# A two-layer sequence block on one core: where the last serial stage and the third mixture of experts stand in the queues, and which engine makes the scan's products

## Chip, cores and metric

One NeuronCore of a Trainium2 chip runs the whole kernel in one launch. The metric is device time in microseconds (us). Matmuls run on TensorE (PE in the profile), activations on ScalarE (ACT), elementwise work and scans on VectorE (DVE) and GpSimd (POOL); SyncE (SP) issues the DMAs.

## The reference, cut to what matters

There are 2048 tokens (2 batches of 1024) of 128 features. Each of four steps adds its output to its input and normalises:

```python
# 1: Mamba: 256 channels, 16 states, per batch
xi, res = split(x @ in_proj_w.T); xi = silu(causal_conv4(xi))
dt, Bm, Cm = split(xi @ x_proj_w.T); delta = softplus(dt @ dt_proj_w.T + dt_b)
h = exp(delta * A) * h + delta * Bm * xi      # along time, 256 x 16 states
y = sum_n(h * Cm) + xi * Dp
x = layernorm(x + (y * silu(res)) @ out_proj_w.T)
# 2: a projection of x rounded to fp8
x = layernorm(x + q(x) @ q(w).T + bias)
# 3: a small state space layer with 16 states for all features
x = layernorm(x + scan16(x) @ C.T + D * x)
# 4: mixture of 8 experts (128 -> 256 -> 128), top 2, capacity 512, and a side network for overflow
x = layernorm(x + moe(x))
```

## The kernel before

The tokens are four chunks (`c` = 0 to 3) of 512. A tile is 128 partitions by 512 tokens of float32. For each chunk there are four stages.

**pre** makes the channels `u`, the gate `res_gate`, the rows of B and C (`low`, written to DRAM and read back by SP, broadcast to 128 partitions, as `b_row` and `c_row`, two states per DMA, in rings of `ROWS` = 4), and `delta`.

**scan**: 32 steps `k` (2 halves of the channels by 16 states). For each step GpSimd makes `drive = du * b_row` (ring of 5), ScalarE writes the decay `exp(delta * rate)` into one of three PSUM banks `ps_state`, VectorE scans in that bank (L919), makes `product = state * c_row` (L934; ring of 5), and in the first chunk of a batch first copies the last column to `carry`. TensorE adds each product into `ps_y` with a matmul by the identity (L475). A float32 matmul is two instructions in the trace.

**tail** is a chain of 16 pieces with hardly any width: gate, output projection (L491), three layer norms, the fp8 projection, the small scan, the router (L534), picking experts. Each piece waits for one on another engine. It uses the PSUM banks `ps_g` and `ps_u`, which the mixture of experts uses as well, so a chunk's tail cannot start before the mixture of experts of the chunk before has ended.

**gate, up, join, down, accum** are the mixture of experts ("MoE"): per expert four groups of three matmuls (L564), Gelu on ScalarE (L774), a product on VectorE (L1079), 16 matmuls (L608) and four accumulations on VectorE (L1092). `fin` is the last layer norm.

The order of the work on every engine is written out: `PLACES` has a place for every piece of every stage, `run` sorts them and calls them in that order, and each engine executes its queue strictly in that order, waiting on semaphores. Before, one set of places serves all chunks (the last chunk has some of its own): while chunk c+1 is scanned, chunk c has its tail and then its MoE. After the last scan stand the last tail, alone, and the last MoE. The last MoE has six PSUM banks, the others three.

The expert weights are split into a high and a low part, and a product is three matmuls of parts: ScalarE makes the high part (L677), VectorE the low part (`split`, L887), 16 instructions on each; before, they are spread over the first scan.

ScalarE loads a table set before an Exp or Ln, a Gelu or a Silu when another set is loaded. The program asks for one by hand in two places (`preload_act_table_set`, L651 and L776); the other loads are placed by the compiler.

Of the kernel before, what the change touches and what calls it, by code (L numbers as in the profile page):

```python
# [15 lines left out]
P = 128  # L16
# [9 lines left out]
RANK = 64  # L26
# [10 lines left out]
DRIVES = 5  # L37
PRODUCTS = 5
# [14 lines left out]
for _k, _w in PARAMS.items():  # L53
# [12 lines left out]
        "pre": (-15.5, -15, -14.75, -12.25, -11.25, -11.25, -11.25, -11),  # L66
        "step": (-0.75, -0.25, 0.25, 0.75, 1.25, 1.75, 2.25, 2.75, 3.25, 3.75, 4.25, 4.75, 5.25, 5.75, 6.25, 6.75, 7.25, 7.75, 8.25, 8.75, 9.25, 9.75, 10.25, 10.75, 11.25, 11.75, 12.25, 12.75, 13.25, 13.75, 14.25, 14.75),
        "fin": (35.5,),
    },
    "tensor": {  # L70
        "pre": (-15.985, -15.243, -15.072, -15.009, -15.009, -14.386, -13.697, -12.945),
        "finish": (1.026, 2.077, 2.38, 4.291, 4.768, 4.895, 4.895, 4.895, 5.341, 5.797, 6.224, 6.906, 7.702, 7.702, 7.702, 7.932, 9.319, 10.249, 10.26, 11.316, 11.443, 11.926, 12.585, 12.638, 12.638, 13.422, 15.593, 15.611, 16.065, 16.065, 16.224, 16.652),
        "tail": (16.789, 18.74, 19.78, 20.114, 20.162, 21.02, 21.662, 21.662, 22.551, 22.551, 22.551, 22.589, 23.318, 23.361, 24.693, 25.257),
        "gate": (23.461, 24.08, 25.461, 26.34, 27.782, 28.281, 29.005, 30.66, 31.128),
        "up": (23.536, 25.234, 26.3, 27.395, 27.991, 28.939, 30.472, 30.681, 31.382),
        "down": (26.054, 26.575, 27.518, 28.046, 29.344, 30.584, 30.786, 32.018, 32.195),
# [4 lines left out]
    },  # L81
    "scalar": {
        "pre": (-15.267, -14.377, -14.369, -14.369, -13.882, -13.064, -12.783, -11.823),
        "step": (-1.07, -1.006, 1.488, 1.488, 1.589, 1.611, 2.1, 2.759, 3.153, 3.566, 5.216, 5.216, 5.248, 5.331, 6.088, 6.923, 7.616, 7.907, 8.049, 8.329, 8.329, 9.344, 9.881, 10.805, 10.879, 10.988, 12.125, 12.63, 13.421, 13.719, 14.454, 14.752),
        "tail": (17.732, 18.093, 18.788, 19.301, 19.58, 19.883, 20.439, 20.816, 21.252, 22.002, 22.002, 22.841, 22.982, 23.694, 25.3, 25.697),
        "gate": (24.049, 24.647, 25.608, 26.597, 28.089, 28.166, 29.618, 30.859, 30.859),
        "fin": (34.6366, 37.5376),
        "split": (-16.891, -3.814, -0.051, 3.661, 5.837, 7.947, 11.702, 14.515),
        "tail 3": (15.02, 17.27, 18.506, 20.73, 21.524, 21.524, 21.524, 22.579, 24.535, 25.601, 25.601, 25.601, 25.601, 25.601, 25.741, 26.135),
        "gate 3": (26.08, 26.08, 29.514, 30.153, 30.779, 30.861, 30.901, 31.003, 31.159),  # L90
    },
    "gpsimd": {
        "du": (-7.973, 6.048),
        "step": (-1.518, -1.379, 0.207, 0.207, 0.207, 1.332, 1.422, 1.422, 1.422, 1.422, 3.619, 3.769, 4.649, 4.649, 5.511, 5.678, 6.659, 8.269, 8.87, 9.084, 9.517, 9.517, 9.517, 9.535, 12.453, 13.427, 13.427, 13.427, 13.427, 13.427, 13.427, 13.427),
        "tail": (17.819, 18.848, 20.618, 21.206, 22.833, 23.004, 25.062, 26.086, 26.086, 27.015, 27.015, 27.015, 27.751, 28.224, 28.256, 28.309),
        "tail 3": (13.509, 13.904, 14.945, 16.762, 17.736, 18.242, 18.307, 19.402, 20.434, 21.642, 24.097, 24.097, 24.097, 24.097, 26.965, 27.136),
    },
    "vector": {
        "delta": (-11.192,),
        "step": STEP,  # L100
        "finish": (0.782, 1.228, 1.228, 2.015, 2.578, 2.578, 3.571, 4.267, 4.782, 4.806, 5.472, 6.005, 6.812, 7.405, 7.681, 8.495, 8.687, 8.826, 9.135, 10.111, 11.059, 11.31, 11.938, 12.367, 12.633, 13.353, 13.353, 14.29, 14.539, 15.174, 15.801, 16.001),
        "gated": (9.428, 16.917),
        "tail": (15.554, 18.289, 18.93, 19.521, 20.126, 20.29, 20.721, 20.862, 22.38, 22.562, 22.562, 22.66, 23.827, 23.988, 24.764, 25.633),
        "join": (24.932, 25.56, 26.732, 28.247, 28.753, 29.639, 30.595, 31.702, 31.923),
        "accum": (26.609, 27.363, 28.477, 29.029, 30.366, 30.691, 31.743, 32.226, 32.579),
        "fin": (34.4726, 38.0196),
        "split": (-0.762, 2.312, 4.875, 11.44, 11.64, 13.773, 14.501, 18.497),
# [19 lines left out]
def build(nc, x_t, params, w_gate, w_up, w_down, bc_dram, out):  # L127
    with ExitStack() as ctx:
# [47 lines left out]
        acc = sb("acc", [P, BLOCKS, P])  # L176
        x1 = sb("x1", [P, BLOCKS, P])
# [5 lines left out]
        l1_ln = l1_abs = gelu[:, 0, 0, :]  # L183
        l1_exp = gelu[:, 0, 1, :]
        l1_relu = gelu[:, 1, 0, :]
        l1_sp = l1_t = gelu[:, 1, 1, :]
        l1_step, l1_decay = gelu[0:STATE, 2, 0, :], gelu[0:STATE, 2, 1, :]
        l1_drive = hidden[0:STATE, 1, 0, :]

# [3 lines left out]
        low = sb("low", [RANK + 2 * STATE, 2, CHUNK])  # L193
        sp_abs = sb("sp_abs", [P, HALVES, CHUNK])
        sp_exp = sb("sp_exp", [P, HALVES, CHUNK])
# [7 lines left out]
        product = sb("product", [P, PRODUCTS, CHUNK])  # L203
        carry = sb("carry", [P, HALVES, STATE])
# [11 lines left out]
        l1_state = sb("l1_state", [STATE, 2, CHUNK])  # L216
# [36 lines left out]
        result = sb("result", [P, BLOCKS, P])  # L253
# [27 lines left out]


# [16 lines left out]
        pre_act = Marks(sem("pre_act"), "u0 u1 gate0 gate1 low abs0 relu0 abs1 relu1 exp0 exp1 ln0 ln1")  # L299
        pre_dve = Marks(sem("pre_dve"), "t0 t1 a0 a1 b0 b1 delta0 delta1")  # L300
# [8 lines left out]
        product_dve = sem("product_dve")  # L309
        y_pe = sem("y_pe")  # L310
# [4 lines left out]
        tail_dve = Marks(sem("tail_dve"), "st1 mo1 sh1 r2 st2 mo2 sh2 t a b sp drive scan st3 mo3 vr msq sh3 inv s3 "  # L315
# [21 lines left out]
        def carries(g):  # L337

            c, k = divmod(g, UNITS)
            return c // PER_BATCH * UNITS + k + 1  # L340
# [4 lines left out]
        def run(engine, **parts):  # L345

            places = PLACES[engine]
            order = sorted((STATE * c + at, c, i, k) for i, kind in enumerate(parts)
                           for c in range(1 if kind == "split" else CHUNKS)
                           for k, at in enumerate(places.get(f"{kind} {c}", places[kind])))  # L350
# [11 lines left out]
        def _(sp):  # L362
# [11 lines left out]
            def pair(m, ring, arrived, row, used):  # L374
# [3 lines left out]
                if m >= ROWS:  # L378
                    sp.wait_ge(used, 2 * (m - ROWS) + 2)
                if r == 0:  # L380
                    sp.wait_ge(rows_out, 16 * (c + 1))
                sp.dma_start(ring[:, m % ROWS, :, :],
                             bc_dram[c % 2, None, row + n:row + n + 2, :].broadcast_to([P, 2, CHUNK])).then_inc(arrived[m % ROWS], 16)

            def pre(c, k):
                if k == 4:
# [5 lines left out]
                    sp.dma_start(bc_dram[c % 2], low[RANK:RANK + 2 * STATE, c % 2, :]).then_inc(rows_out, 16)  # L392

            def step(c, k):
                g = c * UNITS + k
                if g == 0:
                    for m in range(ROWS - 1):
                        pair(m, b_row, b_in, 0, drive_pool)
                        if m < ROWS - 2:
                            pair(m, c_row, c_in, STATE, product_dve)  # L400
                if g % 2 == 0:
                    if g // 2 + ROWS - 2 < STEPS // 2:
                        pair(g // 2 + ROWS - 2, c_row, c_in, STATE, product_dve)
                    if g // 2 + ROWS - 1 < STEPS // 2:
                        pair(g // 2 + ROWS - 1, b_row, b_in, 0, drive_pool)
# [11 lines left out]
        def _(pe):  # L417
# [10 lines left out]
            def pre(c, k):  # L428
                if k == 7:
                    return  # L430
# [26 lines left out]
                else:  # L457
                    h = k - 5
                    after(pe, pre_act, c, "low")
                    last = mm(bank_[:, :], dt_proj[0:RANK, h * P:(h + 1) * P], low[0:RANK, q, :], start=True, stop=True)  # L460
                last.then_inc(pre_pe.sem, 1)

            def finish(c, k):
# [10 lines left out]
                pe.wait_ge(product_dve, g + 1)  # L474
                mm(ps_y[:, :], ident, product[:, g % PRODUCTS, :], start=False, stop=(n == STATE - 1)).then_inc(y_pe, 1)  # L475

            def tail(c, k):
                q = c % 2
                b, t0 = tokens(c)
                if k == 0:  # L480
                    if c:
# [3 lines left out]
                    for j in range(BLOCKS):  # L485
                        t = TAPS - 1 + t0 + j * P
                        mm(block_of(ps_u[1][:, :], j), x_in[:, b, t:t + P], ident, start=(j == 0), stop=False)
# [685 lines left out]
```

## Time and profile before

| | us |
|---|---|
| median of 3 runs (lowest, highest) | 533.63 (529.58, 535.17) |
| the profiled execution's own time | 535.09 |
| its span | 533.3 |
| busy in the span: PE, DVE, ACT, POOL | 425.3, 419.7, 315.1, 178.6 |
| mean granted TensorE clock | 0.889 |

The span is the stretch that the trace covers; the time of the same execution is 1.8 us more. An engine's busy time is the union of its instructions; times in the trace count from the start of the span.

### The profile page before, as it was taken

Reading aid. Unit: us, or ns where it says so; the run is one execution under the profiler, and the core shown is the slowest. Engines: PE = TensorE matmul, PEld = TensorE weight load, DVE = VectorE, ACT = ScalarE, POOL = GpSimd, SP = SyncE. Lnnn points to the kernel's source line nnn. Section 1 sums busy time; section 2 is a strip of 40 time slices with the busy share of each in tenths; the row PEclk is TensorE's granted clock in tenths of the full one; section 3 lists DMA queues with packets and bytes.
Section 4 is the critical chain, followed back from the end, with each engine's and each line's share of the span. In section 5 each row is a group of like instructions: output and inputs, shape, how many; then the busy total and the mean of one; then the engine's idle time right before and its main releaser. Section 6 shows DMA issues by size and latency. Waiting matters only on the chain.

```text
span 533.3 us, 5892 instructions
## 1 busy us (share of the span) xinstructions
PE 425.3 (80%) x1680; PEld 256.9 (48%) x1680; DVE 419.7 (79%) x942; ACT 315.1 (59%) x517; POOL 178.6 (33%) x147
## 2 busy tenths in 40 slices
PE   4976667699649999997569999775599995449994
PEld 3322212253235778552245776432367774147883
DVE  3087999997989999698989989978899884334654
ACT  2586552378738976577578785255787832544232
POOL 0056485555163434234163433451534100000000
PEclk9987977799969999999869999969799998656997
DMA  8295768666426354442193554620835000000000
GB/s 300 109 339 175 240 210 263 211 217 202 163 79 200 116 171 161 142 160 78 32 334 133 180 167 132 220 92 20 323 151 175 23 1 1 20 0 1 0 1 20
DMA packets 22064, 74.18 MB, mean 139 GB/s; under 512 B 2320, under 2 KB 4368, under 8 KB 21648
## 3 DMA queue, kind: packets, MB, share of 16 engines
q1 hardware_dynamic: 22032, 73.82, 41.0%
q8 instruction: 13, 0.21, 0.2%
q14 instruction: 19, 0.16, 0.1%
HBM read 72.50 MB, written 1.31 MB: 138 GB/s over the span
## 4 chain that ended last, share of the span: by engine, by line
PE 50%; DVE 21%; issue 13%; ACT 12%; POOL 2%; DVEq 0%; ACTq 0%; POOLq 0%
PE ps_y L475 12%; PE ps_u L608 9%; PE ps_g L564 8%; DVE ps_state L919 6%; PE ps_u L564 5%; DVE product L934 3%; PE ps_state L564 2%; ACT x L703 2%; ACT ps_state L692 2%; DVE stats L944 1%; PE ps_y L608 1%; POOL drive L813 1%; PE ps_g L523 1%; DVE l_state L990 1%; PE ps_g L534 1%
## 5 line engine op out<-in xcount | busy, mean ns | idle before, releaser
L813 POOL TENSOR_TENSOR drive<-du,b_row 128x512 f32<-128x512 f32 x128 | 164.0, 1290 | 208.3 <-DVE ps_state L919 186.0
L475 PE MATMUL ps_y<-product,par 128*128 128x512 f32 x256 | 135.7, 655 | 13.2 <-DVE product L934 12.9
L692 ACT ACTIVATE ps_state<-delta,decay_rate 128x512 f32<-128x512 f32 x128 | 86.2, 687 | 63.9 <-DVE product L934 61.9
L934 DVE TENSOR_TENSOR product<-ps_state,c_row 128x512 f32<-128x512 f32 x128 | 86.1, 680 | 5.5 <-PE ps_y L475 5.3
L919 DVE TENSOR_TENSOR_SCAN ps_state<-ps_state,carry,drive 128x512 f32<-128x512 f32 x64 | 81.5, 1282 | 4.0 <-ACT ps_state L692 4.0
L475 PEld LDWEIGHTS ps_y<-product,par 128*128 128x128 f32 x256 | 48.9, 208 | 70.6 <-issue 37.3
L919 DVE TENSOR_TENSOR_SCAN ps_state<-ps_state,drive 128x512 f32<-128x512 f32 x64 | 77.3, 1219 | 2.3 <-ACT ps_state L692 2.3
L608 PEld LDWEIGHTS ps_u<-wd,hidden 128*128 128x128 f32 x448 | 54.2, 191 | 5.4 <-issue 2.4
L608 PE MATMUL ps_u<-wd,hidden 128*128 128x128 f32 x448 | 54.6, 275 | 0.0
L1092 DVE SCALAR_TENSOR_TENSOR acc<-ps_u,net_weight,acc 128x128 f32<-128x128 f32 x128 | 35.9, 344 | 15.3 <-PE ps_u L608 12.5
L774 ACT ACTIVATE gelu<-ps_g 128x512 f32<-128x512 f32 (+1 forms) x42 | 24.4, 597 | 31.8 <-PE ps_g L564 18.5
L564 PE MATMUL ps_g<-hn_part,wg 128*128 128x512 f32 x114 | 36.2, 439 | 0.3 <-DVE hidden L1079 0.2
L564 PE MATMUL ps_g<-hn_part,wu 128*128 128x512 f32 x108 | 35.9, 450 | 0.2
L622 ACT ACTIVATE var_log<-moments,eps 128x4 f32<-128x4 f32 x16 | 4.8, 298 | 49.2 <-DVE moments L948 42.4
L774 ACT ACT_TABLE_LOAD x25 | 32.1, 1283 | 0.4
L1079 DVE TENSOR_TENSOR hidden<-gelu,ps_g 128x512 f32<-128x512 f32 x36 | 24.0, 679 | 4.9 <-PE ps_g L564 4.7
L564 PEld LDWEIGHTS ps_g<-hn_part,wu 128*128 128x128 f32 x108 | 20.3, 193 | 11.7 <-issue 5.7
L564 PEld LDWEIGHTS ps_g<-hn_part,wg 128*128 128x128 f32 x114 | 21.1, 196 | 8.7 <-issue 2.9
L692 ACT ACT_TABLE_LOAD x18 | 23.1, 1283 | 0.5 <-DVE carry L930 0.2
L564 PE MATMUL ps_u<-hn_part,wu 128*128 128x512 f32 x63 | 19.6, 420 | 2.2 <-ACT gelu L774 2.2
L802 POOL TENSOR_TENSOR du<-delta,u 128x512 f32<-128x512 f32 x8 | 10.5, 1314 | 31.7 <-DVE delta L908 31.7
L445 PE MATMUL ps_g<-x_in,conv_proj 128*128 128x512 f32 x40 | 20.2, 656 | 0.7 <-ACT conv_proj L625 0.7
(199 smaller groups left out, 605.4 us busy)
## 6 DMA issues: line engine op xcount, KB each, us to landing
b_row<-bc_dram SPq DMA_DIRECT2D x64, 512.0 KB, 5.0
c_row<-bc_dram SPq DMA_DIRECT2D x64, 512.0 KB, 4.1
x_in<-x_t SPq DMA_DIRECT2D x4, 256.0 KB, 7.0
gelu<-w_gate SPq DMA_DIRECT2D x1, 1024.0 KB, 9.3
hidden<-w_up SPq DMA_DIRECT2D x1, 1024.0 KB, 10.9
wd<-w_down SPq DMA_DIRECT2D x1, 1024.0 KB, 12.8
out<-result SPq DMA_DIRECT2D x4, 256.0 KB, 2.4
par<-params SPq DMA_DIRECT2D x1, 598.0 KB, 6.7
```

The costliest lines, as they stand in the source:

```text
L445: last = mm(bank_[:, :], conv_proj[:, k, tap, :], x_in[:, b, t0 + tap:t0 + tap + CHUNK], start=(tap == 0), stop=(tap == TAPS - 1))
L475: mm(ps_y[:, :], ident, product[:, g % PRODUCTS, :], start=False, stop=(n == STATE - 1)).then_inc(y_pe, 1)
L564: last = mm(net_bank(c, e, kind, f)[:, :], w_in[kind][wp][:, e, f * P:(f + 1) * P], hn_parts[hp][:, :], start=(i == 0), stop=(i == 2))
L608: last = mm(block_of(out_bank(c, e)[:, :], j), hidden[:, m % 2, f, j * P:(j + 1) * P], wd[:, e, f, :], start=(f == 0), stop=(f == 1))
L692: nc.scalar.activation(ps_state[g % RING][:, :], delta[:, c % 2, h, :], ACT.Exp, scale=decay_rate[:, h, n:n + 1]).then_inc(decay_act, 1)
L703: last = nc.scalar.activation(out_[:, j, :], of(j), ACT.Identity, bias=shifts[:, j:j + 1], scale=scales[:, j:j + 1])
L774: nc.scalar.activation(gelu[0:rows, m % GROUP, f, :], net_bank(c, e, "wg", f)[0:rows, :], ACT.Gelu).then_inc(gelu_act, inc)
L813: nc.gpsimd.tensor_tensor(drive[:, g % DRIVES, :], du[:, h, :], b_row[:, m % ROWS, n % 2, :], ALU.mult).then_inc(drive_pool, 1)
L919: v.tensor_tensor_scan(state[:, :], state[:, :], drive[:, g % DRIVES, :], 0.0 if first else carry[:, h, n:n + 1], ALU.mult, ALU.add).then_ ...
L934: v.tensor_tensor(product[:, g % PRODUCTS, :], state[:, :], c_row[:, m % ROWS, n % 2, :], ALU.mult).then_inc(product_dve, 1)
L1079: v.tensor_tensor(hidden[0:rows, m % 2, f, :], gelu[0:rows, m % GROUP, f, :], net_bank(c, e, "wu", f)[0:rows, :], ALU.mult).then_inc(hidde ...
L1092: last = v.scalar_tensor_tensor(acc[:, j, :], block_of(out_bank(c, e)[:, :], j), net_weight[:, j, e:e + 1], acc[:, j, :], ALU.mult, ALU.add)
```

## The change

- The banks of the last chunk's tail are no longer `ps_g` and `ps_u` but the scan's `ps_state` and `ps_y` (`tail_bank`), and its scratch tiles lie in the ring of products (`l1_of`). It need no longer wait for the third MoE. In the new order the third MoE (c = 2) stands after the last scan, interleaved piece by piece with the last tail; the last MoE follows.
- A quarter of the products (steps 3, 7, 11, ... of every chunk) is made by GpSimd: there the scan writes its result into `drive` in SBUF, and GpSimd multiplies, and in chunks 0 and 2 copies the carry.
- In chunks 1 and 2 GpSimd adds the products of steps 2i and 2i+1, so TensorE adds one tile for two steps.
- The ring of drives has 6 tiles instead of 5, that of products 8 instead of 5. To make room, `low`, `sp_exp` and `l1_state` have one buffer instead of two and `result` shares `acc`. The softplus of `pre` is done for one half of the channels after the other.
- A whole new order, with places of its own for every chunk. All splits of the weights now stand ahead of the first scan, on ScalarE and VectorE. `gate`, `up` and `join` are placed by half of an expert.
- Table sets are asked for ahead of each activation that needs Exp or Ln instead of at two places: 168 requests instead of 14.

```diff
-DRIVES = 5
-PRODUCTS = 5
+DRIVES = 6
+PRODUCTS = 8
+ODD = frozenset(range(1, UNITS, 2))
+PAIRED = (NONE, ODD, ODD, NONE)
+QUARTER = frozenset(range(3, UNITS, 4))
+MULTIPLIED = (QUARTER, QUARTER, QUARTER, QUARTER)
...
+        def tail_bank(c, name):
+            if c == LAST:
+                return {"r1": ps_state[0], "x1t": ps_state[1], "ffn": ps_state[2], "x2t": ps_y, "dlt": ps_state[2],
+                        "bx": ps_state[0], "mean": ps_state[1], "r3": ps_y, "hnt": ps_state[2], "logits": ps_state[1],
+                        "counts": ps_y}[name]
...
             def finish(c, k):          # TensorE
-                pe.wait_ge(product_dve, g + 1)
+                if absorbed(g):
+                    return
+                if paired(g):
+                    pe.wait_ge(pair_pool, count(paired, g))
+                else:
+                    made(pe, g)
...
             def tail(c, k):            # TensorE
                 if k == 0:
-                    if c:
+                    if c == LAST:
+                        pe.wait_ge(product_dve, count(by_vector, STEPS - 1))
+                        pe.wait_ge(state_dve, STEPS)
+                    elif c:
...
             def step(c, k):            # ScalarE
                 if old >= 0:
-                    act.wait_ge(product_dve, old + 1)
-                    if old // UNITS % PER_BATCH == 0:
-                        act.wait_ge(carry_dve, carries(old))
+                    if multiplied(old):
+                        act.wait_ge(state_dve, old + 1)
+                    else:
+                        made(act, old)
...
+                nc.scalar.preload_act_table_set(EXP_LN)
                 nc.scalar.activation(ps_state[g % RING][:, :], delta[:, c % 2, h, :], ACT.Exp,
...
+            def multiply(c, k):        # GpSimd
+                pool.wait_ge(state_dve, g + 1)
+                pool.wait_ge(c_in[m % ROWS], 16 * (m // ROWS + 1))
+                if g >= PRODUCTS:
+                    added(pool, g - PRODUCTS)
+                nc.gpsimd.tensor_tensor(product[:, g % PRODUCTS, :], drive[:, g % DRIVES, :], c_row[:, m % ROWS, n % 2, :],
+                                        ALU.mult).then_inc(product_pool, 1)
+                if c % PER_BATCH == 0:
+                    nc.gpsimd.tensor_copy(carry[:, h, n:n + 1], drive[:, g % DRIVES, CHUNK - 1:CHUNK]).then_inc(carry_pool, 1)
+
+            def pair(c, k):            # GpSimd
+                made(pool, g - 1)
+                made(pool, g)
+                nc.gpsimd.tensor_tensor(product[:, g % PRODUCTS, :], product[:, (g - 1) % PRODUCTS, :],
+                                        product[:, g % PRODUCTS, :], ALU.add).then_inc(pair_pool, 1)
...
             def step(c, k):            # VectorE
-                v.tensor_tensor_scan(state[:, :], state[:, :], drive[:, g % DRIVES, :],
+                v.tensor_tensor_scan(drive[:, g % DRIVES, :] if multiplied(g) else state[:, :], state[:, :], drive[:, g % DRIVES, :],
...
             def finish(c, k):          # VectorE
+                if multiplied(g):
+                    return
```

Here `made(eng, g)` waits for the product of step g from whichever engine makes it, and `added(eng, g)` until it has been used. What the new places give, as the order of the queues: on TensorE and VectorE, scan 0 whole, then tail 0 beside steps 3 to 22 of scan 1, MoE 0 up to step 5 of scan 2, tail 1 beside steps 11 to 30 of scan 2, MoE 1 up to step 14 of scan 3, tail 2 beside the rest of scan 3, then tail 3 beside MoE 2, then MoE 3. Between two products GpSimd makes three or four drives. On ScalarE, activations with Exp or Ln and those with Gelu or Silu alternate 67 times in the whole program (65 before), 13 of them from the start of tail 3 to the start of MoE 3.

## Rows read from the trace of the kernel before

**Rows 1.** Busy time by stage; after the stretch its length, then the engines
```profile
32.00:117.00 85.00, 61.66 (x111) 22.48 (x110) 80.73 (x128) 45.03 (x68) 54.13 (x43) 0.84 0.71 239
117.00:230.00 113.00, 98.83 (x414) 60.84 (x413) 100.14 (x207) 79.45 (x123) 45.77 (x36) 0.94 0.46 150
230.00:337.00 107.00, 94.00 (x408) 59.19 (x407) 97.51 (x235) 77.00 (x125) 42.80 (x35) 0.94 0.48 161
337.00:444.00 107.00, 86.80 (x392) 56.13 (x390) 93.13 (x199) 66.16 (x108) 34.40 (x27) 0.92 0.33 116
444.00:481.00 37.00, 17.25 (x65) 10.58 (x64) 12.95 (x52) 16.41 (x41) 1.09 (x1) 0.61 0.02 7
481.00:533.30 52.30, 44.24 (x250) 36.43 (x250) 26.63 (x93) 16.27 (x30) 0.00 (x0) 0.86 0.02 6
```

**Rows 2.** Timeline: last gating of the scan, first expert matmuls after the last tail
```profile
443.35 0.69 DVE L940 TENSOR_TENSOR res_gate<-res_gate,ps_y 128x512 f32<-128x512 f32 x1 [0.79 <-PE ps_y L475]
...
480.86 1.65 PE L564 MATMUL ps_u<-hn_part,wg 128*128 128x512 f32 x3 [0.28 <-DVE logits L1014]
```

**Rows 3.** Groups by line, VectorE and TensorE
```profile
L934 DVE TENSOR_TENSOR product<-ps_state,c_row 128x512 f32<-128x512 f32 x128 | 86.1, 680 | 5.5 <-PE ps_y L475 5.3
L919 DVE TENSOR_TENSOR_SCAN ps_state<-ps_state,carry,drive 128x512 f32<-128x512 f32 x64 | 81.5, 1282 | 4.0 <-ACT ps_state L692 4.0
L930 DVE COPY carry<-ps_state 128x1 f32<-128x1 f32 x64 | 9.5, 148 | 0.1
L475 PE MATMUL ps_y<-product,par 128*128 128x512 f32 x256 | 135.7, 655 | 13.2 <-DVE product L934 12.9
```

**Rows 4.** The expert layers' matmuls (L564, then L608) in the third MoE's stretch
```profile
337.00:444.00 107.00, 28.34 (x96) 17.29 (x96) 0.92 0.33 116
337.00:444.00 107.00, 15.57 (x128) 15.52 (x128) 0.92 0.33 116
```

**Rows 5.** One line each: products of experts, accumulations, small scan, all on VectorE
```profile
L1079 DVE TENSOR_TENSOR hidden<-gelu,ps_g x36: 673/678/690, 170.1 to 518.6; 128x512 f32<-128x512 f32 x36
...
L1092 DVE SCALAR_TENSOR_TENSOR acc<-ps_u,net_weight,acc x128: 327/344/353, 181.0 to 526.5; 128x128 f32<-128x128 f32 x128
...
L990 DVE TENSOR_TENSOR_SCAN l_state<-gelu,hidden x2: 1211/1600/1990, 149.7 to 370.3; 16x512 f32<-16x512 f32 x2
```

**Rows 6.** GpSimd: its drives by duration, and the waits for them
```profile
L813 POOL TENSOR_TENSOR drive<-du,b_row x128: 1257/1271/2177, 34.3 to 416.7; 128x512 f32<-128x512 f32 x128
...
POOL drive L813 <- DVE ps_state L919: 186.0, 83, 8.4
POOL drive L813 <- DMA b_row<-bc_dram: 21.7, 5, 9.7
```

**Rows 7.** The splits' durations on VectorE, and a shared moment in the timeline
```profile
L887 DVE SCALAR_TENSOR_TENSOR wg<-gelu,par,wg x8: 452/464/1490, 33.0 to 121.7; 128x256 fp32r<-128x256 f32 x8
L887 DVE SCALAR_TENSOR_TENSOR wu<-hidden,par,wu x8: 473/1477/1482, 34.4 to 122.1; 128x256 fp32r<-128x256 f32 x8
...
34.31 5.19 POOL L813 TENSOR_TENSOR drive<-du,b_row 128x512 f32<-128x512 f32 x4
34.44 1.48 DVE L887 SCALAR_TENSOR_TENSOR wu<-hidden,par,wu 128x256 fp32r<-128x256 f32 x1
```

**Rows 8.** Timeline of the start: first splits, softplus, first scan
```profile
12.86 0.51 ACT L677 ACTIVATE wg<-gelu,par 128x256 fp32r<-128x256 f32 x1 [2.20 <-DMA gelu<-w_gate]
20.16 0.69 ACT L622 ACTIVATE u<-ps_g,par 128x512 f32<-128x512 f32 x1 [2.30 <-PE ps_g L445]
28.55 0.95 DVE L898 TENSOR_SCALAR delta<-sp_exp 128x512 f32<-128x512 f32 x2 [16.48 <-ACT sp_exp L622]
35.84 2.47 DVE L919 TENSOR_TENSOR_SCAN ps_state<-ps_state,drive 128x512 f32<-128x512 f32 x2
```

**Rows 9.** Table loads: the decays' line, and one load with its follower in the timeline
```profile
L692 ACT ACT_TABLE_LOAD x18 | 23.1, 1283 | 0.5 <-DVE carry L930 0.2
...
36.69 1.28 ACT L692 ACT_TABLE_LOAD   x1
37.99 0.69 ACT L692 ACTIVATE ps_state<-delta,decay_rate 128x512 f32<-128x512 f32 x1
```

**Rows 10.** Chain that ended last: the second chunk's tail begins, its MoE begins
```profile
231.18 1.79 PE ps_u L491 x16
...
284.02 0.97 PE ps_g L564 x3
```

More of the change, by code:

```diff
@@ L88 @@
-        "split": (-16.891, -3.814, -0.051, 3.661, 5.837, 7.947, 11.702, 14.515),
-        "tail 3": (15.02, 17.27, 18.506, 20.73, 21.524, 21.524, 21.524, 22.579, 24.535, 25.601, 25.601, 25.601, 25.601, 25.601, 25.741, 26.135),
-        "gate 3": (26.08, 26.08, 29.514, 30.153, 30.779, 30.861, 30.901, 31.003, 31.159),
+        "pre 0": (0, 1.0256, 1.2308, 1.641, 2.0513, 2.6667, 2.8718, 3.0769, 3.2821),
+        "split": (0.2051, 0.4103, 0.6154, 0.8205, 1.4359, 1.8462, 2.2564, 2.4615),
[19 rows of a table added]
     },
     "gpsimd": {
-        "du": (-7.973, 6.048),
@@ L97 @@
     },
     "vector": {
[L99 to L107, printed above, removed]
[3 rows of a table removed]
+        "tail 0": (0, 12.7719, 13.4737, 13.614, 14.4561, 14.7368, 14.8772, 16.5614, 17.1228, 17.5439, 17.8246, 18.1053, 18.9474, 19.0877, 19.3684, 19.9298),
+        "split": (0.1404, 0.2807, 0.4211, 0.5614, 0.7018, 0.8421, 0.9825, 1.1228),
[31 rows of a table added]
@@ L182, in build @@
                     "wu": hidden[:, :, :, :].rearrange("p r f (e n) -> p (r f e) n", n=HIDDEN)}
[L183 to L188, printed above, removed]
+        L1_NAMES = "abs exp relu sp step decay drive"
         u = sb("u", [P, 2, HALVES, CHUNK])
         res_gate = sb("res_gate", [P, 2, HALVES, CHUNK])
-        low = sb("low", [RANK + 2 * STATE, 2, CHUNK])
+        low = sb("low", [RANK + 2 * STATE, CHUNK])
         sp_abs = sb("sp_abs", [P, HALVES, CHUNK])
-        sp_exp = sb("sp_exp", [P, HALVES, CHUNK])
+        sp_exp = sb("sp_exp", [P, CHUNK])
         sp_ln = sp_abs
@@ L203, in build, with l1_of @@
         product = sb("product", [P, PRODUCTS, CHUNK])
+        def l1_of(c, name):
+            name = {"ln": "abs", "t": "sp"}.get(name, name)
+            i = L1_NAMES.split().index(name)
+            if c == CHUNKS - 1:
+                place = product[:, i, :]
+            elif i < 6:
+                place = gelu[:, i // 2, i % 2, :]
+            else:
+                place = hidden[:, 1, 0, :]
+            return place[0:STATE, :] if name in ("step", "decay", "drive") else place
         carry = sb("carry", [P, HALVES, STATE])
@@ L335, in block_of, with multiplied, absorbed, count @@
             return ap[:, j * P:(j + 1) * P]
-        def carries(g):
-            c, k = divmod(g, UNITS)
-            return c // PER_BATCH * UNITS + k + 1
+        def multiplied(g):
+            return g % UNITS in MULTIPLIED[g // UNITS]
+        def absorbed(g):
+            return g % UNITS + 1 in PAIRED[g // UNITS]
+        def count(which, g):
+            return sum(map(which, range(g + 1)))
+        def by_pool(g):
+            return multiplied(g)
+        def by_vector(g):
+            return not multiplied(g)
+        def summed(g):
+            return not absorbed(g)
+        def paired(g):
+            return g % UNITS in PAIRED[g // UNITS]
+        def made(eng, g):
+            if multiplied(g):
+                eng.wait_ge(product_pool, count(by_pool, g))
+            else:
+                eng.wait_ge(product_dve, count(by_vector, g))
+        def added(eng, g):
+            if absorbed(g):
+                eng.wait_ge(pair_pool, count(paired, g + 1))
+            else:
+                eng.wait_ge(y_pe, count(summed, g))
+        def carried(eng, g):
+            which = by_pool if multiplied(g) else by_vector
+            eng.wait_ge(carry_pool if multiplied(g) else carry_dve,
+                        sum(which(i) for i in range(g + 1) if i // UNITS % PER_BATCH == 0))
         def blocks_of(ap):
@@ L459, in pre @@
                     after(pe, pre_act, c, "low")
-                    last = mm(bank_[:, :], dt_proj[0:RANK, h * P:(h + 1) * P], low[0:RANK, q, :], start=True, stop=True)
+                    last = mm(bank_[:, :], dt_proj[0:RANK, h * P:(h + 1) * P], low[0:RANK, :], start=True, stop=True)
                 last.then_inc(pre_pe.sem, 1)
@@ L539, in tail @@
                     after(pe, tail_dve, c, "picked")
+                    after(pe, tail_act, c, "x3")
                     for j in range(BLOCKS):
[L541 removed]
+                        o = tail_bank(c, "counts")[:, j * EXPERTS:(j + 1) * EXPERTS]
                         mm(o, before[:, :], picked[:, j, :], start=True, stop=False)
@@ L821, in tail @@
                                             ALU.add).then_inc(tail_pool.sem, 1)
-            run("gpsimd", du=make_du, step=step, tail=tail)
+            def multiply(c, k):
+                g = c * UNITS + k
+                h, n = divmod(k, STATE)
+                m = g // 2
+                if not multiplied(g):
+                    return
[8 more added lines that the diff above has]
+            def pair(c, k):
+                g = c * UNITS + k
+                if not paired(g):
+                    return
+                made(pool, g - 1)
+                made(pool, g)
+                nc.gpsimd.tensor_tensor(product[:, g % PRODUCTS, :], product[:, (g - 1) % PRODUCTS, :],
+                                        product[:, g % PRODUCTS, :], ALU.add).then_inc(pair_pool, 1)
+            run("gpsimd", du=make_du, step=step, multiply=multiply, pair=pair, tail=tail)
         @block.vector
@@ L985, in tail @@
                 if k == 8:
                     after(dve, tail_act, c, "decay")
-                    do(tail_dve, v.tensor_tensor(l1_drive[:, :], l1_step[:, :], ps_u[1][0:STATE, :], ALU.mult))
+                    do(tail_dve, v.tensor_tensor(l1_of(c, "drive"), l1_of(c, "step"), tail_bank(c, "bx")[0:STATE, :], ALU.mult))
                     own(tail_dve, c, "drive")
                     first = c % PER_BATCH == 0
-                    do(tail_dve, v.tensor_tensor_scan(l1_state[:, q, :], l1_decay[:, :], l1_drive[:, :],
-                                                      0.0 if first else l1_state[:, 1 - q, CHUNK - 1:CHUNK],
-                                                      ALU.mult, ALU.add))
+                    if c:
+                        after(dve, tail_pe, c - 1, "r3")
@@ L993, in tail @@
+                    if not first:
+                        own(tail_dve, c - 1, "keep")
+                    do(tail_dve, v.tensor_tensor_scan(l1_state[:, :], l1_of(c, "decay"), l1_of(c, "drive"),
+                                                      0.0 if first else l1_carry[:, :], ALU.mult, ALU.add))
+                    own(tail_dve, c, "scan")
+                    do(tail_dve, v.tensor_copy(l1_carry[:, :], l1_state[:, CHUNK - 1:CHUNK]))
                 if k == 9:
                     after(dve, tail_pe, c, "r3")
-                    layer_norm_stats(tail_dve, c, lambda j: block_of(ps_g[0][:, :], j), "st3", "mo3")
+                    layer_norm_stats(tail_dve, c, lambda j: block_of(tail_bank(c, "r3")[:, :], j), "st3", "mo3")
```

278 lines of the change are left out of this document (145 added, 133 removed), and 113 rows, old and new, of the table PLACES.

## Prediction

> **What bounds the kernel now.** I read the busy time by stage first [rows 1]. The first scan lasts 85 us, of which DVE is busy 80.7 (95%). Then come three stretches of 113, 107 and 107 us in which one chunk is scanned while the chunk before has its tail and its MoE: DVE is busy 89, 91 and 87% of them, PE 87, 88 and 81%. So the middle is bound by DVE's work, with PE close behind; neither waits long for one thing. Two stretches are different. From 444 to 481 us only the last tail runs: DVE is busy 13 us, PE 17, the granted clock falls to 0.61. From 481 on only the last MoE runs, PE busy 44 of 52 us. The timeline gives the serial stage's ends exactly: the last gating of the scan at 443.35, the first expert matmuls at 480.86 [rows 2]. These 37 us have an empty PE, and that is what the change fills. GpSimd is nowhere a limit: before 83 of its 128 drives it waits for a scan, 186 us in all [rows 6]. At the start VectorE stands idle 16.5 us until the first softplus arrives [rows 8].
>
> I cost the new order as four stretches and compare each with its counterpart.
>
> **Start (was 32 us).** All 16 splits now stand ahead of the first scan. VectorE does them in its idle 16.5 us [rows 8]. ScalarE has 12 more of them (2 before 20 us stay) of 0.51 us in the middle of `pre`, 6 to 7 us, against gaps such as the 2.30 us before the second `u` [rows 8]; some 3 us remain. The softplus done half by half gives back about 2: one half's four passes come before the other's instead of alternating with it. The first scan begins 0 to 3 us later; I take 1. The new wait in the second half of the softplus (for the first half's second pass on VectorE) holds only ScalarE's own queue and lies in this estimate. Start: 33 us.
>
> **Middle (was 412 us, DVE busy 371.5 as the sum of the first four stretches [rows 1]).** From DVE's busy time go:
> - the third MoE, moved behind the last scan: 17 products of 0.68 and 36 accumulations of 0.344 (about 0.28 apart as they overlap) [rows 5], 11.5 + 10.3 = 21.8;
> - 32 products, at 86.1/128 = 0.67 each [rows 3], 21.5;
> - 16 carry copies, which lie nearly wholly under their neighbours (their group says 0.148 each, the extra time is some 0.05), 0.8;
> - 16 splits: 8 at mostly 0.46, 8 at mostly 1.48 [rows 7], about 14.
>
> What is left is 313 us. A scan that writes to SBUF isn't in the trace at this size. The nearest row is the small scan, 1.21 to 1.99 us [rows 5], against 1.28 in PSUM [rows 3]; so 32 of them cost 0 to 23 us more, and as the small scan's lower end equals the normal one, I take 0.
>
> The port term: a split with two SBUF inputs took 1.48 us where it started just after a drive on GpSimd (34.44 after 34.31) and 0.46 at other times [rows 7]. GpSimd gets 64 more instructions, so what VectorE does with two SBUF inputs (six delta passes and about four in a tail per chunk) meets it more often: 0 to 40 times 1.0 us, and I take 5. The Trainium skill says in "SBUF — State Buffer", section "Who interferes with whom", that a VectorE instruction with two SBUF inputs contends with a GpSimd instruction that reads SBUF, and that the second one waits for the first to finish. The split's two durations agree; by that rule alone each meeting could cost up to a whole GpSimd instruction, which would take the sum some 12 us higher.
>
> So DVE has 318 us. The first scan's part is 80.7 less the splits' 14 and 8 products, 61 us, and runs at 95% as before: 64. The other 257 us I take at 90%, one above the mean of the three stretches, as PE has less to do: 286. Middle: 350 us, to 383. With PE: its 341 us [rows 1] lose the third MoE (28.3 + 15.6 for the experts [rows 4], about 3 for side network and counts, 47) and 32 of 128 additions to `ps_y` at 135.7/128 = 1.06 [rows 3], 34. That leaves 260, or 75% of the stretch: not the bound, save where a MoE stands beside a scan. With GpSimd: per four steps of chunks 1 and 2 it has 4 drives, 1 product, 2 sums, 7 times 1.28 = 9.0 us; VectorE's pace there is 257/96 x 4 = 10.7 us. It fits, with 1.7 us to spare. Behind a `multiply` that waits for a scan stand the next drives; three or four drives are made ahead, some 5 us of VectorE's work, which covers it. The new sums at the end of a chunk delay the gating by about two GpSimd instructions, 2.5 us, beside other work in chunks 1 and 2. SP waits for GpSimd's products with its `c_row` loads and the next `b_row` load stands behind; 0 to the 21.7 us that drives wait for `b_row` now [rows 6]; the ring holds 8 steps, so I take 0.
>
> **Last tail beside the third MoE (was 37 us).** PE's work: 47 of the MoE and the tail's 17.25 at a clock of 0.61 [rows 1], which is about 11 at full clock: 58. The chain's own length: 37, plus table loads, as tail and MoE alternate on ScalarE: six of the 13 loads stand ahead of a piece of the tail, 6 x 1.28 [rows 9] = 8, plus waits behind expert matmuls. With a scan beside it a tail took from 231.2 to 284.0, 53 us [rows 10]. Both ways some 55 to 60; I take 60, with 50 and 80 as ends (80: the two nearly one after the other, 37 + 47). A table load is followed at once by its activation, 36.69 + 1.28 to 37.99 [rows 9]. The Trainium skill speaks against this mixing: "ScalarE: Activation LUTs", section "What ACT_TABLE_LOAD costs", adds a drain of about 1380 ns to every switch. The row shows none; by the page the 13 switches would make this stretch 18 us longer.
>
> **Last MoE (was 52.3 us).** It is unchanged but starts with a busy PE. Its first matmuls took 1.65 us for three [rows 2] at the low clock; the later ones run about 0.84. I take off 3: 49.
>
> **Table requests.** 168 instead of 14. The trace has 128 decays and 18 loads on their line [rows 9]: no load where the set is there already. But those are placed by the compiler, and every request by hand before stood where a load was needed; whether a needless request becomes a load isn't shown. Bounds: 0 and 135 x 1.283 us of ScalarE. I take 0, the nearer to the decays' row.
>
> **Sum.** 33 + 350 + 60 + 49 = 492 us of span. The execution's own time is 1.8 more, 494; that of before lies 1.5 above the median of the runs, so 492 as a median.
>
> **Rivals.**
> - GpSimd sets the pace (0.12). Its queue is in order and now waits for products as well as scans; if the waits exceed the spare 1.7 us per four steps by about as much as one more instruction (1.28 us) in the 16 groups of chunks 1 and 2, that is +20: 512. For: its load doubles per step there, 83 drives wait for scans now. Against: the deeper rings.
> - The last two stages take turns (0.08): 80 instead of 60, 512. For: in-order queues, a chain with 11 pieces on PE. Against: the tail got through a scan's queue in 53.
> - Slower (0.08): every request issues its load. Then each decay costs ScalarE 0.69 + 1.28 = 1.97 us, and up to the last scan it has 267 us [rows 1], less 15 for the third MoE, plus 130 x 1.28 = 167: 419 against DVE's 318. At 95% that is 441 instead of 350; with 33, 58 and 49 the sum is 581. It decides as soon as more than some 60 of the needless loads are real.
> - The shift does nothing (0.04): the middle loses its overlap (the MoEs of chunks 0 and 1 against fewer scan steps) and gives back the 42 us, within 1% of before.
>
> The forecast has 0.68. Its own range, from the unknown terms (0 to 3, 0 to 23, 0 to 40, DVE at 88 to 94%, 50 to 66), taken together and not all at one end, is 474 to 508. The overall range goes to 520 for the first two rivals. A difference under 1% can't be told from none here. Faster 0.88, same 0.04, slower 0.08.
>
> **What would show it.** The last gating near 383 us; the middle's DVE at 90% or more; PE busy and its clock above 0.85 between the last gating and the last MoE, this stretch near 60 us; 16 splits at 0.46 us ahead of the first scan; 192 instructions that add to `ps_y` instead of 256; GpSimd near 262 us busy; 67 table loads. Wrong if table loads are 200; if VectorE's scans wait for drives; if the stretches with a MoE beside a scan are set by PE and the last gating comes after 400.

## The result and the profile after

The changed kernel took 607.74 us (605.83 to 608.72, 4 runs) against 532.87: the ratio is 1.141, 95% interval 1.134 to 1.148. I had forecast 492 (474 to 520). It came out on the side of the third rival: every request for a table set became a load. Two executions further down, one of e3 (569.17 us) and one of e6 (589.63), ran at a granted clock of 0.70 against 0.84 to 0.88 in the others of the same kernel, and the medians and ratios leave them out.

The page of the changed kernel, busy time by engine:

```profile
PE 419.0 (69%) x1616; PEld 248.7 (41%) x1616; DVE 411.0 (68%) x898; ACT 496.0 (82%) x654; POOL 259.4 (43%) x227
```

and its groups of table loads on ScalarE by line (L851 is the request ahead of a decay, L857 ahead of a reciprocal root, L824 of a softplus; L941 and L776 are placed by the compiler):

```profile
L851 ACT ACT_TABLE_LOAD x128 | 164.2, 1283 | 17.7 <-DVE product L1126 15.4
L941 ACT ACT_TABLE_LOAD x25 | 32.1, 1283 | 0.4
L857 ACT ACT_TABLE_LOAD x20 | 25.7, 1283 | 24.5 <-DVE moments L1140 14.1 <-DVE moments L1305 8.5 <-DVE mean_sq L1198 1.6
L776 ACT ACT_TABLE_LOAD x9 | 11.5, 1283 | 1.1 <-POOL eps L959 1.0
L824 ACT ACT_TABLE_LOAD x8 | 10.3, 1283 | 0.7 <-DVE delta L1093 0.6
L895 ACT ACT_TABLE_LOAD x4 | 5.1, 1283 | 0.1
L903 ACT ACT_TABLE_LOAD x4 | 5.1, 1283 | 0.1
L924 ACT ACT_TABLE_LOAD x4 | 5.1, 1283 | 1.5 <-DVE centred L1219 1.5
```

That is 202 loads, and 168 of them are exactly the requests: 128 + 20 + 8 + 4 + 4 + 4. Before, 18 loads stood on the decays' line [rows 9]. ScalarE went from 315 to 496 us busy. A stretch of ScalarE's timeline in the changed kernel's first scan:

```profile
103.64 1.28 ACT L851 ACT_TABLE_LOAD   x1
104.94 0.69 ACT L852 ACTIVATE ps_state<-delta,decay_rate 128x512 f32<-128x512 f32 x1
105.64 1.28 ACT L851 ACT_TABLE_LOAD   x1
106.94 0.69 ACT L852 ACTIVATE ps_state<-delta,decay_rate 128x512 f32<-128x512 f32 x1
```

The reader is to see that nothing stands between the rows: one decay each 2.00 us, with no wait. The same set is loaded again and again. The waits of VectorE (`ps_state L1109` and `drive L1109` are the scans that write to PSUM and to SBUF; after the colon the us in total, how often, the longest):

```profile
DVE ps_state L1109 <- ACT ps_state L852: 38.8, 39, 3.0
...
DVE drive L1109 <- ACT ps_state L852: 25.0, 14, 5.7
```

VectorE's scans waited 64 us for decays; before, 4.0 us for one half of the scans (rows 3) and 2.3 for the other. In this trace the first scan starts at 39.41, the last gating at 502.98 and the last MoE's first matmuls at 555.93. By stretch, cut within a few us of these, with the columns of rows 1:

```profile
36.00:503.00 467.00, 300.63 (x995) 161.95 (x993) 333.31 (x640) 413.53 (x512) 254.88 (x217) 0.78 0.42 140
503.00:554.00 51.00, 48.62 (x300) 38.20 (x300) 31.57 (x101) 36.58 (x61) 1.10 (x1) 1.00 0.00 1
554.00:606.90 52.90, 43.24 (x266) 35.80 (x266) 28.98 (x108) 23.29 (x44) 0.00 (x0) 0.93 0.03 11
```

In the first, ScalarE is 89% busy and VectorE 71%: another engine bounds the scans. The granted clock is 0.78 there, against 0.91 between 36 and 444 us before, and TensorE is busy 64% of it (83% before). The second stretch is as I wanted it: the serial tail, 37 us with TensorE at 47% in [rows 1], now shares some 53 us with the third MoE, with TensorE at 95% and a clock of 1.00.

### The profile page after: what moved, and what is told of

The parts are those of the page before. It is cut to its first block, busy times and chain, and to the rows that moved or that the text cites. A ratio compares the mean times of both kernels' runs of the same rounds, so it can differ in the third digit from the quotient of the medians.

```text
span 606.9 us, 6086 instructions
## 1 busy us (share of the span) xinstructions
PE 419.0 (69%) x1616; PEld 248.7 (41%) x1616; DVE 411.0 (68%) x898; ACT 496.0 (82%) x654; POOL 259.4 (43%) x227
## 4 chain that ended last, share of the span: by engine, by line
ACT 25%; PE 17%; DVE 9%; issue 6%; DVEq 0%; ACTq 0%
ACT L851 9%; PE ps_g L717 4%; ACT ps_state L852 4%; PE ps_u L762 4%; ACT L857 3%; PE ps_u L717 2%; PE ps_state L717 1%; ACT L941 1%; DVE acc L1293 1%; PE ps_y L762 1%; DVE ps_state L1109 1%; DVE product L1126 1%; ACT gelu L941 1%; ACT acc L864 1%; ACT L776 1%
## 5 line engine op out<-in xcount | busy, mean ns | idle before, releaser
L851 ACT ACT_TABLE_LOAD x128 | 164.2, 1283 | 17.7 <-DVE product L1126 15.4
L624 PE MATMUL ps_y<-product,par 128*128 128x512 f32 x192 | 111.9, 706 | 27.8 <-DVE product L1126 16.6
L852 ACT ACTIVATE ps_state<-delta,decay_rate 128x512 f32<-128x512 f32 x128 | 88.5, 692 | 1.5
L1002 POOL TENSOR_TENSOR product<-drive,c_row 128x512 f32<-128x512 f32 x32 | 41.0, 1282 | 87.5 <-DVE drive L1109 87.5
L1109 DVE TENSOR_TENSOR_SCAN ps_state<-ps_state,carry,drive 128x512 f32<-128x512 f32 x48 | 61.5, 1285 | 24.5 <-ACT ps_state L852 24.4
L1109 DVE TENSOR_TENSOR_SCAN ps_state<-ps_state,drive 128x512 f32<-128x512 f32 x48 | 58.5, 1225 | 20.2 <-ACT ps_state L852 14.5
L624 PEld LDWEIGHTS ps_y<-product,par 128*128 128x128 f32 x192 | 39.3, 221 | 79.9 <-DVE product L1126 29.9
L1126 DVE TENSOR_TENSOR product<-ps_state,c_row 128x512 f32<-128x512 f32 x96 | 63.8, 677 | 0.0
L1014 POOL TENSOR_TENSOR product<-product 128x512 f32<-128x512 f32 x32 | 40.6, 1269 | 44.0 <-DVE product L1126 43.2
L762 PE MATMUL ps_u<-wd,hidden 128*128 128x128 f32 x448 | 55.1, 276 | 1.6 <-DVE hidden L1280 0.9
L857 ACT ACT_TABLE_LOAD x20 | 25.7, 1283 | 24.5 <-DVE moments L1140 14.1
L941 ACT ACTIVATE gelu<-ps_g 128x512 f32<-128x512 f32 (+1 forms) x42 | 24.8, 596 | 24.4 <-PE ps_g L717 17.2
L717 PE MATMUL ps_g<-hn_part,wu 128*128 128x512 f32 x108 | 33.9, 428 | 0.5 <-ACT gelu L941 0.5
L941 ACT ACT_TABLE_LOAD x25 | 32.1, 1283 | 0.4
L1109 DVE TENSOR_TENSOR_SCAN drive<-ps_state,drive 128x512 f32<-128x512 f32 x16 | 19.4, 1215 | 18.7 <-ACT ps_state L852 18.7
L965 POOL TENSOR_TENSOR du<-delta,u 128x512 f32<-128x512 f32 x8 | 10.1, 1268 | 44.9 <-DVE delta L1098 44.5
```

Of the source, the lines that this page charges most:

```text
L717: last = mm(net_bank(c, e, kind, f)[:, :], w_in[kind][wp][:, e, f * P:(f + 1) * P], hn_parts[hp][:, :], start=(i == 0), stop=(i == 2))
L762: last = mm(block_of(out_bank(c, e)[:, :], j), hidden[:, m % 2, f, j * P:(j + 1) * P], wd[:, e, f, :], start=(f == 0), stop=(f == 1))
L851: nc.scalar.preload_act_table_set(EXP_LN)
L852: nc.scalar.activation(ps_state[g % RING][:, :], delta[:, c % 2, h, :], ACT.Exp, scale=decay_rate[:, h, n:n + 1]).then_inc(decay_act, 1)
L857: nc.scalar.preload_act_table_set(EXP_LN)
L941: nc.scalar.activation(gelu[0:rows, m % GROUP, f, :], net_bank(c, e, "wg", f)[0:rows, :], ACT.Gelu).then_inc(gelu_act, inc)
```

## The experiments

The kernel before was measured again beside the experiments: 531.79 us beside e1, e3, e4 and e5, 532.53 beside e6, e7, e9 and e10. The ratios are against these, and can differ from the quotient of the medians by half a per cent.

Theory A: the change lost by its needless table loads alone, and without them it would be the gain forecast. Rival B: the new order, with GpSimd's work and the single buffers, is slow in itself and ScalarE's loads fill time that was idle.

**e1_loads_once: the change, with loads only where needed.**

```diff
+            def need(name):
+                if name != table[0] and name == EXP_LN:
+                    nc.scalar.preload_act_table_set(EXP_LN)
+                table[0] = name
...
-                nc.scalar.preload_act_table_set(EXP_LN)
+                need(EXP_LN)
```

and `need("silu")` or `need("gelu")` ahead of those activations. As the queue is written in order, a Python variable knows the loaded set.

> The kernel after the change, but ScalarE asks for the Exp and Ln table set only where another set is loaded: 67 loads instead of 202; queues, banks and all else as in the changed kernel. Theory A (every needless request issues its load, 135 x 1.283 = 173 us of ScalarE, and this alone turned the change): 480 to 510 us, ScalarE busy near 323 us, last gating of the scan near 385. Rival B (the new order, with GpSimd's waits and single buffers, is slow in itself): 530 to 580 us, VectorE's scans still wait for something else.

Measured: 505.46 us, ratio to before 0.948 (0.943 to 0.952), so 102 us less than the changed kernel. Its page and loads:

```profile
PE 402.7 (80%) x1616; PEld 243.1 (48%) x1616; DVE 418.9 (83%) x898; ACT 316.8 (63%) x519; POOL 264.6 (52%) x227
```

```profile
L779 ACT ACT_TABLE_LOAD x33 | 42.3, 1283 | 14.6 <-DVE moments L1315 7.7 <-DVE product L1136 6.1 <-DVE moments L1150 0.3
L951 ACT ACT_TABLE_LOAD x25 | 32.1, 1283 | 0.6 <-issue 0.2
L783 ACT ACT_TABLE_LOAD x9 | 11.5, 1283 | 2.1 <-PE ps_u L643 1.0 <-POOL eps L969 1.0
```

67 loads. ScalarE's 496 us fell by 179, VectorE is at 83%. The last gating moved from 502.98 to 399.45, by 103.5 us: the whole difference lies ahead of it. B has fallen as what turned the change. Theory A holds for the loss, not for the full gain: the kernel gains 26 us where 41 were forecast.

**e4_before_loads: the kernel before, plus a request ahead of each decay.**

```diff
+                nc.scalar.preload_act_table_set(EXP_LN)
                 nc.scalar.activation(ps_state[g % RING][:, :], delta[:, c % 2, h, :], ACT.Exp,
```

> The kernel before, plus a request for the Exp and Ln table set ahead of each of the 128 decays, nothing else. Theory A: 110 more loads (18 at decays are needed anyway), 141 us more of ScalarE; slower than 533 by 50 to 110 us. Rival B: ScalarE has room (315 of 533 us busy), under 15 us slower.

Measured: 597.26 us, ratio 1.119 (1.115 to 1.123). By line there are 175 loads, 110 more, for 65 us. Nothing else differs, so the requests alone hurt the old order too:

```profile
L692 ACT ACT_TABLE_LOAD x128 | 164.2, 1283 | 16.6 <-DVE product L935 12.7 <-DVE delta L909 1.7
```

**e6_half_loads and e7_decays_once: how much each load costs.** In e6 every second decay's request is always issued, in e7 the 40 requests that are not at decays (`need(EXP_LN, True)` there, which asks whatever is loaded). The edit of e6:

```diff
+                if k % 2 and table[0] == EXP_LN:
+                    nc.scalar.preload_act_table_set(EXP_LN)
                 need(EXP_LN)
                 nc.scalar.activation(ps_state[g % RING][:, :], ...
```

> As e1_loads_once (505 us, 67 loads), but at every second decay the request is issued always: 118 loads, 51 more, 65 us more of ScalarE, all in the scans. If the cost is in proportion (102 us for 135 loads), 544 us. If ScalarE's room in the middle (235 of 364 us busy in e1_loads_once) takes up the first of them, the curve is bent: 505 to 525 us here, and most of the 102 us comes with the second half.

> The opposite split: requests ahead of decays only where needed, all 40 others issued always: 96 loads, 29 more than e1_loads_once, 37 us more of ScalarE, most of them in the tails' chains. By proportion 527 us. If only the decays' loads matter (a scan step needs 1.97 us of ScalarE), under 10 us more than e1_loads_once.

Measured: e6 540.72 us (ratio 1.014, 1.010 to 1.018), e7 527.57 (0.989, 0.983 to 0.996). Together with the two ends:

| kernel | loads | us | us per load over e1 |
|---|---|---|---|
| e1_loads_once | 67 | 505.5 | |
| e7_decays_once | 96 | 527.6 | 0.76 |
| e6_half_loads | 118 | 540.7 | 0.69 |
| the change | 202 | 607.7 | 0.76 |
| e4 over before | 175 over 65 | 597.3 | 0.60 |

The curve is close to straight: e7's 29 loads, which stand in the softplus and the tails, and e6's 51, at decays, cost about as much apiece as all 135. If the costs of e6 and e7 simply add up, the 55 loads that neither has cost 0.82 us each, so the last ones are if anything dearer. ScalarE was idle for a third of e1's middle (235 of 364 us busy), and that took up only about two fifths to a half of each load's 1.28 us. In e6 and e7 the cost doesn't come through TensorE's clock: from 36 to 400 us it was granted at 0.83 in e1, 0.83 in e7 and 0.85 in e6. In the changed kernel it was 0.78, and what that adds to the last loads isn't separated. Even my rival, "it decides as soon as more than some 60 are real", was wrong in this: 29 already cost 22 us.

**e5_tail_alone: the last tail out of cover.** Same banks and scratch tiles, but all pieces of the last tail and the last MoE stand behind the third MoE.

```diff
+            def late(kind, c):
+                return 64 if c == LAST and kind in ("tail", "gate", "up", "down", "join", "accum", "fin") else 0
-            order = sorted((STATE * c + at, c, i, k) ...
+            order = sorted((STATE * c + at + late(kind, c), c, i, k) ...
```

> As e1_loads_once, but the whole last tail (and so the last MoE) stands behind the third MoE in every queue, in the same banks and scratch tiles as in the change. If the overlap of tail and MoE is what gains: slower than e1_loads_once by 25 to 37 us (36 us of serial tail come out of cover, less the loads that no longer alternate). Rival: under 10 us, because the tail beside the MoE stretched the MoE by as much as it hid.

Measured: 537.13 us, ratio to before 1.009 (1.005 to 1.013); 31.7 over e1, although e5 has only 55 table loads, 12 fewer. The timelines of e1, then of e5, at the last MoE's first matmuls:

```profile
399.45 0.69 DVE L1142 TENSOR_TENSOR res_gate<-res_gate,ps_y 128x512 f32<-128x512 f32 x1
...
452.23 1.65 PE L717 MATMUL ps_u<-hn_part,wg 128*128 128x512 f32 x3
```

```profile
446.34 2.98 PE L646 MATMUL ps_state<-par,res_gate 128*128 128x128 f32 x16
...
483.66 1.65 PE L720 MATMUL ps_u<-hn_part,wg 128*128 128x512 f32 x3 [0.28 <-DVE logits L1227]
```

From the last gating (400.05 in e5) the third MoE takes 46 us alone and the tail 37 more; overlapped both are done in 53. This overlap is worth more than the whole 26 us by which e1 beats before: without it the new order is 1% behind the old. In e5 the third MoE is done and the last tail's projection starts at 446.34; before, the last gating, just ahead of the tail, stood at 443.35. So all other parts of the change together gained nothing ahead of the tail.

**e3_no_quarter: all products back on VectorE**, each of the moved ones right behind its scan.

```diff
-MULTIPLIED = (QUARTER, QUARTER, QUARTER, QUARTER)
+MULTIPLIED = (NONE, NONE, NONE, NONE)
```

> As e1_loads_once, but all products on VectorE, those of steps 3, 7, ... placed right behind their scans. If VectorE's work sets the middle, 32 products of 0.67 us give 15 to 25 us more than e1_loads_once. Rival (GpSimd in its own queue is the limit): same or faster by up to 10 us.

The carry copies that GpSimd had made go back with them, and all scans write to PSUM again. Measured: 511.93 us, ratio 0.958 (0.952 to 0.963): 6.5 over e1, with intervals that touch at 0.952, so the gain of the moved products is only just resolved. The last gating came at 406.3. Less than expected: VectorE was only 10 us busier, for 32 products of 0.67 us = 21 (see below on the port).

**e9_pe_twice and e10_no_sums: the two sides of the pairs.** e9 adds each pair's sum twice; e10 has no sums and drops the first product of each pair, whose tile counts as free as soon as it is made. (VectorE waited only 0.9 us for a free product tile in e1, so this last point is worth little.) The main lines, with comments put in here:

```diff
+                if paired(g):                      # e9, TensorE
+                    mm(ps_y[:, :], ident, product[:, g % PRODUCTS, :], start=False, stop=False)
                 mm(ps_y[:, :], ident, product[:, g % PRODUCTS, :], ...
```

```diff
-                if paired(g):                      # e10, TensorE; GpSimd makes no sum
-                    pe.wait_ge(pair_pool, count(paired, g))
-                else:
-                    made(pe, g)
+                made(pe, g)
```

> As e1_loads_once, but in chunks 1 and 2 TensorE adds each pair's sum twice, so its instructions are as many as without pairs, with GpSimd's sums kept (what is computed differs: those sums count double). If TensorE's relief of 34 us is a gain of the change: 10 to 25 us slower than e1_loads_once. If VectorE alone sets the middle (341 of 364 us busy): under 5 us.

> As e1_loads_once, but GpSimd makes no sums of pairs and TensorE adds only the second product of each pair in chunks 1 and 2 (left out: the first product of each pair). GpSimd has 42 us less. If GpSimd's reads hold up VectorE's instructions with two SBUF inputs (delta passes of 1.63 instead of 0.69 us), these get shorter on the mean and the time falls by 5 to 12 us. If GpSimd's load costs nothing: within 2 us of e1_loads_once.

Measured: e9 516.36 us (ratio 0.968, 0.960 to 0.976), 10.9 over e1; e10 496.32 (0.929, 0.923 to 0.935), 9.1 under it. So TensorE's relief is worth about 11 us and GpSimd's sums cost about 9: what the pairs bring can't be told from nothing. In e9 the additions to `ps_y` took 139 us of TensorE (101.1 + 38.1) instead of 106.2, about the 34 us that I had counted as relief, but TensorE as a whole was only 13 us busier: the granted clock was 0.906 instead of 0.866 (0.906 to 0.922 in its four executions, 0.863 to 0.876 in e1's), and its other matmuls took 20 us less. Read the other way round, of the 33 us that the pairs took off TensorE some 20 came back, because its other matmuls ran at a lower granted clock. Why the clock was lower, no run here separates. VectorE's delta passes, all 128x512 with two inputs in SBUF, in e1 and then in e10:

```profile
L1103 DVE TENSOR_TENSOR delta<-sp_exp,delta 128x512 f32<-128x512 f32 x8 | 11.3, 1416 | 0.3
L1105 DVE TENSOR_TENSOR delta<-delta,sp_relu 128x512 f32<-128x512 f32 x8 | 8.4, 1048 | 0.3
L1108 DVE TENSOR_TENSOR delta<-delta,sp_abs 128x512 f32<-128x512 f32 x8 | 7.3, 907 | 0.3
```

```profile
L1099 DVE TENSOR_TENSOR delta<-sp_exp,delta 128x512 f32<-128x512 f32 x8 | 8.5, 1063 | 0.3
L1101 DVE TENSOR_TENSOR delta<-delta,sp_relu 128x512 f32<-128x512 f32 x8 | 7.4, 929 | 0.3
L1104 DVE TENSOR_TENSOR delta<-delta,sp_abs 128x512 f32<-128x512 f32 x8 | 6.5, 810 | 0.3
```

Before, each took 0.68 us. A stretch of e1's timeline shows how a pass comes to take longer:

```profile
72.96 2.93 POOL L991 TENSOR_TENSOR drive<-du,b_row 128x512 f32<-128x512 f32 x2
73.00 1.77 DVE L1103 TENSOR_TENSOR delta<-sp_exp,delta 128x512 f32<-128x512 f32 x1
74.80 1.64 DVE L1105 TENSOR_TENSOR delta<-delta,sp_relu 128x512 f32<-128x512 f32 x1
76.47 0.69 DVE L1108 TENSOR_TENSOR delta<-delta,sp_abs 128x512 f32<-128x512 f32 x1
```

The first pass starts 0.04 us after a drive on GpSimd, the second during the next drive; the third, after both drives have ended at 75.89, takes 0.69 us.

A version of e1 without pairs, with every product added by itself, wasn't tried. Nor do the parts add up: the overlap's 32 us, the moved products' 6.5 and the pairs' 2 make 40, and e1 gains 26. The other parts of the change, the deeper rings, the single buffers, the splits ahead of the first scan and the places as such, have no run of their own; that they cost the difference is not shown.

## Why the prediction was wrong, point by point

**Table requests: the step that failed.** I took 0 from the bounds "0 and 135 x 1.283 us", as "nearer to the decays' row". That row counts loads placed by the compiler and says nothing on requests, as I wrote myself. The right end was the upper one: 202 loads. 135 of them were needless. By e1 the term was worth 102 us, not 0, and it turned a gain of 5% into a loss of 14%. With it the premise of the middle fell, that VectorE's work bounds the scans: ScalarE did. A chance of 0.08 for it had no row behind it. When a term has bounds of 0 and 173 us and no row between them, it has to be in the range.

**The rival's size.** I gave 581 us. Measured 607.7. Its loads (202) and ScalarE's busy time before the last gating (419 forecast, 413.5 measured) were right. (The sum has 58 for the last tail's stretch where the forecast has 60; it makes no difference.) The error is mostly ScalarE at 95% of the middle: it was 89%, 467 us instead of 441.

**The rest is tested by e1**, which is the change as I forecast it, 505.5 against 492. That it lies within the 474 to 508 of the forecast is partly luck: the middle came 16.5 us late, and the last tail's stretch 7 us short took some of that back.

- Start: first scan near 36.8 forecast, 37.65 measured. The splits took 0.48 us each, ahead of the first scan. Right.
- Middle: last gating 399.5 instead of 383. VectorE was 340.8 us busy between 36 and 400, not 318, but at 94% instead of 91. The port term was mis-sized. The rule of the Trainium skill that I weighed ("SBUF — State Buffer", "Who interferes with whom") is borne out by e1: in its rows by line the delta pass L1103 has min/median/max of 0.69/1.63/1.77 us, and the timeline above shows it beside the drives. No meeting of it cost more than 1.08 us, less than a GpSimd instruction of 1.28. Excess over 0.68 and 0.69 in the delta passes (8 x 1.33 = 10.6 for the three above, 2.3 for the first pass) and in the small state space layer's passes, which took up to 1.63 us instead of 0.69 (7), makes 20 us, where I took 5; the some 12 us more that the prediction gives by that rule alone were nearer to it. About 8 us more busy time I haven't traced in full; some 3 of them are small instructions that grew too, such as a 128x4 one from 0.22 to 0.35 us, 12 times.
- Scans that write to SBUF: 1.21 and 1.27 us, as in PSUM. Right.
- TensorE not the bound of the middle: only half right. e9 gives it back 64 instructions and loses 11 us. I had counted 260 us busy at the clock of before; e1 has 284 from 36 to 400. As an estimate, busy time by granted clock, that is the same work: 260 x 0.91 = 237 and 284 x 0.83 = 236. The work was right, and the lower clock was not in the sum. That it matters where a MoE stands beside a scan is my reading, not tested.
- GpSimd's pace: it waits for VectorE's scans in e1 too (25.4 us before drives, 186 before [rows 6]). No scan of e1 has a wait for a drive listed, so its drives don't hold the scans up. Its sums cost 9 us by e10, where VectorE is also 9.7 us less busy; how much of it is VectorE's longer passes and how much the sums' own delay isn't separated.
- Last tail beside the MoE: 60 forecast, 52.8 measured. TensorE was busy 55.1 of the 57 us from 400 to 457, at a clock of 0.97, so its work sets this stretch. I had put that work at 58, with the MoE's 47 read at a clock of 0.92, and added waits behind expert matmuls that didn't come.
- Last MoE: 49 forecast, 52.2 measured. The granted clock was 1.00 from 440 to 450, then 0.83, and 0.53 from 452.2 to 455, so its first three matmuls took 1.65 us again, as in rows 2, although TensorE had been busy 3.0 of the 4 us up to 450 and all of the time from there on; from 455 on it was back at 1.00 for 20 us. TensorE was busy 42.1 us of the stretch instead of 44.2, but idle 10.1 instead of 8.1. In the changed kernel the first three took 0.97 us, and this stretch still lasted 51.0, only 1.3 less than before, where I took off 3.
- The rule on a drain after a table load (Trainium skill, "ScalarE: Activation LUTs", "What ACT_TABLE_LOAD costs"): no run shows one. In the changed kernel's timeline a load of 1.28 us is followed after 1.30 by its activation, and ahead of its 128 decays ScalarE is idle 1.5 us in all. Most of these load the same set again, but a real switch shows no gap either, as here in e1 from Exp to Gelu:

```profile
452.96 0.23 ACT L783 ACTIVATE exps<-centred 128x32 f32<-128x32 f32 x1
453.20 1.28 ACT L951 ACT_TABLE_LOAD   x1
454.50 0.60 ACT L951 ACTIVATE gelu<-ps_u 128x512 f32<-128x512 f32 x1
```

## What to carry to other kernels

Count a hint to the compiler as an instruction until a trace shows that it costs nothing; here a `need()` of four lines in Python, that knows the loaded set, is worth 102 us. A load on an engine with a third of its time idle still cost 0.6 to 0.76 us of its 1.28: "this engine has room" doesn't make its work free. I read this as the decays' place in a ring of three banks between two other engines; no run changes the ring, and e7's loads stand outside it. Moving work to GpSimd has a second price, on VectorE's instructions with two SBUF inputs, and here it ate nearly what the pairs gave. Covering the serial tail with matmuls that were ready was the part that paid, 32 us; the moved products gave 6.5. And work taken off TensorE can come back in part as a lower granted clock: read the clock beside the busy time.

## What the runs showed of the hardware that I had not expected

A table load that is asked for by hand isn't skipped when the set is there already: 135 of the 202 loads in the changed kernel, 1283 ns each; in the timeline above each loads the set that was loaded 2 us before. VectorE's pass with one SBUF tensor input and two constants (L1101 in e1) stretched as well, from 0.43 us at the median to 1.40 at most.

The kernel e1_loads_once, at 505.5 us, is 5% under the kernel before and 17% under the changed one. e10 is lower still, but leaves out half of the products of two chunks.
